# Round 0 of a token mixer with experts: peak, reciprocal and first spread of batch 3's state ahead of batch 1's correction on VectorE, the quadrant swap ahead of a transpose on TensorE

## What is computed

```python
h = relu(causal_conv(fake_quant(emb)[x]))                  # width 2
h = h + scan_mixer(layernorm(h))                           # below
h = h + expert_mlp(layernorm(h))                           # attn, fc1, gelu, fc2, next, gelu
...
log_x = log_matmul_exp(log_x0_I, log_cum)                  # linear recurrence x_t = A x_(t-1) + B u_t
c = jnp.max(log_x.real, axis=-1, keepdims=True)
x = jnp.exp(log_x - c + 2).real.reshape(Bsz, L, n * d)     # 4 heads of 64
y = jnp.matmul(x, C) + jnp.matmul(u, D)
```

## Time and profile before

| | us |
|---|---|
| median of 3 runs | 171.41 (171.39 to 171.44) |
| profiled execution, its time | 171.2 |
| its span | 169.5 |
| TensorE (matmul) busy | 160.5, 95% of the span |
| VectorE busy | 128.4, 76% |
| ScalarE busy | 101.7, 60% |
| GpSimd busy | 101.7, 60% |
| mean granted TensorE clock | 0.999 |

### The profile page before, as it was taken

One profiled execution on the slowest core, in us unless ns is written; L12 is line 12 of the kernel. 1 busy time (PEld: TensorE's weight loads), 2 busy tenths in 40 slices (PEclk: granted clock), 3 DMA queues, 4 the chain that ended last, 5 costly groups with the idle time before them and its releaser, 6 DMA issues.

```text
span 169.5 us, 3498 instructions
## 1 busy us (share of the span) xinstructions
PE 160.5 (95%) x1165; PEld 138.1 (81%) x1165; DVE 128.4 (76%) x403; ACT 101.7 (60%) x238; POOL 101.7 (60%) x168
## 2 busy tenths in 40 slices
PE   5977989999999999999999979999999999989992
PEld 1666875897765799987669979999999999989991
DVE  3979959833338384897995998989979898649893
ACT  3048999452233532423426947959779597788991
POOL 5337777669997134460313783996969969785000
PEclk9999999999999999999999999999999999999999
DMA  4996000000000000000000000010010100110022
GB/s 140 353 429 296 4 0 2 0 6 0 0 0 4 0 0 0 0 6 0 0 0 0 4 0 0 0 68 0 0 68 0 64 0 4 62 62 6 0 106 82
DMA packets 2182, 7.47 MB, mean 44 GB/s; under 512 B 238, under 2 KB 748, under 8 KB 1908
## 3 DMA queue, kind: packets, MB, share of 16 engines
q1 hardware_dynamic: 2146, 7.23, 11.2%
q10 hardware_dynamic: 18, 0.02, 0.1%
HBM read 5.15 MB, written 2.10 MB: 43 GB/s over the span
## 4 chain that ended last, share of the span: by engine, by line
PE 81%; DVE 6%; ACT 5%; POOL 3%; issue 3%; DMA 1%; POOLq 0%; ACTq 0%; DVEq 0%
PE bank L1358 12%; PE bank L1338 11%; PE bank L1287 8%; PE bank L1202 6%; PE bank L1196 5%; PE bank L1284 4%; PE bank L1066 4%; PE bank L1116 4%; PE bank L1307 4%; PE bank L1122 3%; PE bank L1314 2%; PE bank L1091 2%; PE bank L1039 2%; PE bank L1168 2%; DVE st L784 2%
## 5 line engine op out<-in xcount | busy, mean ns | idle before, releaser
L519 POOL TENSOR_TENSOR hid_p<-hid_f,hid_p 128x256 fp32r<-128x256 f32 x48 | 34.2, 739 | 14.2 <-ACT hid_p L713 14.2
L711 ACT ACTIVATE hid_f<-bank,pa 128x256 f32<-128x256 f32 x64 | 30.8, 491 | 15.6 <-PE bank L1338 14.2
L1338 PE MATMUL bank<-xaT_p,fc_p 128*128 128x256 f32 x192 | 35.0, 293 | 0.2 <-issue 0.2
L1358 PE MATMUL bank<-hid_p,out_hi 128*128 128x256 f32 x128 | 32.3, 289 | 0.5 <-POOL hid_p L519 0.5
L1338 PEld LDWEIGHTS bank<-xaT_p,fc_p 128*128 128x128 f32 x192 | 26.6, 189 | 0.4 <-issue 0.3
L1358 PEld LDWEIGHTS bank<-hid_p,out_hi 128*128 128x128 f32 x128 | 23.4, 188 | 1.3 <-POOL hid_p L519 0.7
L713 ACT ACTIVATE hid_p<-bank,pa 128x256 fp32r<-128x256 f32 x48 | 23.4, 487 | 0.0
L1287 PE MATMUL bank<-pb,xh 128*128 128x128 f32 x128 | 19.5, 275 | 0.0
L533 POOL TENSOR_TENSOR rstd<-spread,neg_half 128x8 f32<-128x8 f32 x8 | 13.6, 1696 | 8.9 <-DVE spread L976 8.9
L1358 PE MATMUL bank<-hid_p,out_lo 128*128 128x256 f32 x64 | 17.8, 278 | 0.0
L1287 PEld LDWEIGHTS bank<-pb,xh 128*128 128x128 f32 x128 | 16.9, 192 | 0.0
(11 more groups left out here) (161 smaller groups left out, 373.7 us busy)
## 6 DMA issues: line engine op xcount, KB each, us to landing
fc_w<-in_fc SPq DMA_DIRECT2D x2, 2048.0 KB, 11.7
out<-res SPq DMA_DIRECT2D x7, 256.0 KB, 2.0
pa<-in_pack_a SPq DMA_DIRECT2D x1, 407.0 KB, 3.2
pb<-in_pack_b SPq DMA_DIRECT2D x1, 384.0 KB, 4.5
out<-res SPq DMA_DIRECT2D x2, 128.0 KB, 1.7
pw<-in_pack_a SPq DMA_DIRECT2D x1, 64.0 KB, 3.8
emb_w<-in_emb SPq DMA_DIRECT2D x1, 62.5 KB
conv_w<-in_conv ACTq DMA_DIRECT2D x1, 1.0 KB
```

The source lines that it names most:

```text
L519: nc.gpsimd.tensor_tensor(hid_p[1][:, half, c, :], hid_f[:, m % HID_SLOTS, :], hid_p[0][:, half, c, :].bitcast(F32), ALU.subtract).then_in ...
L711: full = nc.scalar.activation(hid_f[:, m % HID_SLOTS, :], src, ACT.Gelu, bias=bias)
L1338: last = mm(fc1_bank(8 * b + n)[:, 0:HALF], fc1_p[w][:, e * HID + c * P:e * HID + (c + 1) * P], xaT_p[m][:, b % 2, half, :], start=(k == 0 ...
L1358: last = mm(out_bank(b, half)[:, half * HALF:(half + 1) * HALF], out_p[w][:, e, c * CH:(c + 1) * CH], hid_p[m][:, half, c, :], start=(c == ...
```

## The change

In round 0 alone, VectorE makes the peak, the reciprocal and the first of the two spreads of batch 3 right behind its maxima, ahead of the correction of batch 1's attended values. The second spread and the two scalings stay where they were. TensorE makes the swap of batch 3 ahead of the transposes of xa of batch 1. All other rounds stay as they are; the code of the three instructions is taken into two small functions. No instruction is added or removed.

```diff
--- before.py
+++ after.py
@@ -895,6 +895,22 @@
                                                     hid_p[0][:, half, c, :].bitcast(F32),
                                                     ALU.subtract).then_inc(hid_lo_dve, 1)
 
+                def reciprocals(b):
+
+                    if b == 0:
+                        dve.wait_ge(fc1_split, NE)
+                    dve.wait_ge(amax_ready, b + 1)
+                    dve.wait_ge(swap_done, b + 1)
+                    nc.vector.tensor_tensor(peak[:], amax[:, b % 2], bank_sw.rearrange("p (a i) -> p a i", a=NP),
+                                            ALU.max).then_inc(peak_ready, 1)
+                    dve.wait_ge(peak_ready, b + 1)
+                    chained(nc.vector.reciprocal(rcp[:], peak[:]))
+
+                def spread_reciprocal(a):
+
+                    return nc.vector.transpose(bank[a][:].rearrange("p (i k) -> p i k", k=NCH),
+                                               rcp[:, a, :].unsqueeze(2).broadcast_to([P, T, NCH]))
+
                 def late_residual(o):
 
                     dve.wait_ge(gel_ready, o + 1)
@@ -942,6 +958,9 @@
                                                            apply_absolute_value=True, apply_transpose=True)
                         last.then_inc(amax_ready, 1)
                     scan_part(j, "maxima")
+                    if j == 0:
+                        reciprocals(3)
+                        spread_reciprocal(0)
                     high_parts(j, range(0, 2))
                     if j == NB - 1:
                         late_residual(NB - 3)
@@ -980,18 +999,12 @@
                     b = j + 3
                     if b < NB:
                         g, bb = divmod(b, GB)
-                        if b == 0:
-                            dve.wait_ge(fc1_split, NE)
-                        dve.wait_ge(amax_ready, b + 1)
-                        dve.wait_ge(swap_done, b + 1)
-                        nc.vector.tensor_tensor(peak[:], amax[:, b % 2], bank_sw.rearrange("p (a i) -> p a i", a=NP),
-                                                ALU.max).then_inc(peak_ready, 1)
-                        dve.wait_ge(peak_ready, b + 1)
-                        chained(nc.vector.reciprocal(rcp[:], peak[:]))
+                        if j != 0:
+                            reciprocals(b)
                         scan_part(j, "reciprocal")
                         for a in range(NP):
-                            last = nc.vector.transpose(bank[a][:].rearrange("p (i k) -> p i k", k=NCH),
-                                                       rcp[:, a, :].unsqueeze(2).broadcast_to([P, T, NCH]))
+                            if (j, a) != (0, 0):
+                                last = spread_reciprocal(a)
                         chained(last)
                         scan_part(j, "spread")
                         if b >= 2:
@@ -1386,6 +1399,8 @@
                     fill(j, 1)
                     if j < 0:
                         fill(j, MIXER)
+                    if j == 0:
+                        swap_quadrants(scaled)
                     if 0 < attended < NB:
                         transpose_xa(attended)
                     if 0 <= mixed < NB:
@@ -1393,7 +1408,7 @@
                         mixer_out(mixed, 3)
                     if attended == 0:
                         transpose_xa(0)
-                    if scaled < NB:
+                    if scaled < NB and j != 0:
                         swap_quadrants(scaled)
                     fill(j, 2)
                     fill(j, 3)
```

## The result

| | before | changed |
|---|---|---|
| median, first timing (5 runs each) | 171.44 | 170.46 (170.03 to 170.71) |
| profiled execution | 171.2 | 170.71 |
| its span | 169.5 | 169.0 |

Two later executions, one of the kernel before and one of run 2, took some 885 us where all others took 169 to 174; they are left out of every comparison.

What follows compares the result with a forecast made beforehand. TensorE was taken as the bound from 100 us on, held ahead of that by its wait for xh; the stall's 1.19 us less 0.38 for late transposes of h gave 0.8 us won, 170.6 us, range 170.35 to 171.05.

Steps and rivals of the forecast that it cites:

- The stall's price: End of round 0: TensorE's wait for xh with its restart costs 3.35 - 2.16 = 1.19 us, the most to win.
- The delay of the transposes of h: Round 0: VectorE's correction starts 0.38 us later, and TensorE's transposes of h move one for one, to 93.57.
- The sum: End of round 0: 1.19 - 0.38 = 0.81 us won, TensorE's first mixer product for batch 3 at about 97.74.
- What sets the end: End of round 0: xh is ready by about 97.74, so TensorE's own lateness, not xh, sets the end.
- The swap without a wait on TensorE: Round 0: the swap, moved to 90.31, finds the maxima over at 89.80, with 0.5 us to spare.
- Its price on ScalarE's path: Round 0: the swap makes the xa transposes and ScalarE's reading of them 0.14 us later.
- L975's hold: VectorE's variance spread, 0.71 us, is held by GpSimd's subtraction; starting later it is held less, and L976's end stays.
- The lower bound: If the hand-over from swap to correction were hidden, 1.19 - 0.14 = 1.05 us would be won: 170.36 us.
- Its other term: Lower bound: with the hand-over hidden, only ScalarE's 0.14 us would remain as the delay.
- B: Moved instructions or next round cost more, VectorE held by GpSimd or xa transposes waiting: 170.9 to 171.1; chance 0.14.
- C: Gain taken back at the end, in round 5, by TensorE's wait for GpSimd's subtraction: no change, 171.4; chance 0.09.
- D: GpSimd's L519 series holds VectorE repeatedly, TensorE starts the mixer 0.4 us after today: 171.85; chance 0.05.

Runs made afterwards that it cites:

- run 2: The kernel before with only TensorE's half, the swap ahead of the xa transposes in round 0: 171.23 us against 171.43, ratio 0.9988.
- runs 8 and 10: The changed kernel with GpSimd's subtraction 3 ahead of its power in rounds 1 to 4, timed twice: 170.20 and 170.17 us, ratios 0.9930 and 0.9929.
- run 7: The changed kernel with the first spread moved behind the addition into h, ahead of its statistics: 170.52 us, ratio 0.9948 to the kernel before.
- run 3: The changed kernel with both spreads of batch 3 ahead of the correction in round 0: 170.93 us, ratio 0.9975 to the kernel before.
- run 6: The changed kernel with the swap back at its old place, so only VectorE's half: 172.19 us, ratio 1.0064 to the kernel before.
- run 4: The changed kernel with only peak and reciprocal ahead, both spreads behind the statistics: 170.59 us, ratio 0.9954 to the kernel before.
- run 12: Changed kernel, GpSimd's subtraction 3 first in rounds 1 to 4, round 0's swap behind the xa transposes, first spread behind the addition: 170.15 us, ratio 0.9920.
- run 5: The kernel before, unaltered, timed against itself and profiled again: 171.46 us against 171.48, ratio 1.0001.
- run 9: The changed kernel unaltered, a third time, against the kernel before: 170.43 us, ratio 0.9940.

## Why the prediction was right and wrong

Two terms of the sum failed, the price of the stall and the delay of the transposes of h; the mechanism, TensorE's own lateness and not xh, is the one that the runs show.

- **The stall's price: too small.** The step took 1.19 us, with a later round as the unheld measure (2.16). In three profiles of the changed kernel the distance is 2.09, 2.04 and 2.05 us, 2.06 on average, and in the two profiles of before it is 3.35 and 3.32, so the stall and its restart cost 1.27 us. The reference round had a wait of its own, for GpSimd, too short for the list of waits; runs 8 and 10 took it away, and the distance there fell to 2.08 to 2.10.
- **The delay of the transposes of h: too large.** The step said 0.38; it is 0.25, three times to the hundredth (4.94 against 4.69). The hand-over from swap to peak took 0.41, not 0.46, the first spread 0.64 to the next start, not 0.66; the correction started 0.30 late instead of 0.38, and its pair took 0.05 less, as the statistics did in run 7, which also stand right behind a spread there (0.83 against 0.87).
- **The sum** 1.27 - 0.25 = 1.02 us is what the traces give from the maxima to the end (81.01 on average against 79.98). Two small errors, 0.08 and 0.13, both to the low side, made 0.8 of it. All timed executions together, 17 of the changed kernel and 76 of before, have medians of 170.29 and 171.45: 1.16. The 0.1 us between 1.03 and 1.16 is not explained by any stretch of the profiles; it may be the scatter ahead of round 0, but the profiles do not show it: the maxima start at 88.72 on average in the three with VectorE's old order, at 88.69 in the other eleven. The ratio of the first timing, 1.2 us, lies high in the same way. With the 1.03 of the traces alone the median would be 170.38, just inside the range, so the two terms explain about half of the way from the forecast of 170.6 to 170.18; the other 0.2 us stays open.
- **What sets the end: right.** Xh was there first, and TensorE came late by the delay of h. With a delay of 0.25, 1.0 (run 3) and 2.04 us (run 6) the traces give a gain of 1.03, 0.35 and -0.77 us to the end of the span; 1.27 less the delay is 1.02, 0.27 and -0.77.
- **The swap without a wait on TensorE: right**, at 90.69 with the maxima over at 90.18. Its price on ScalarE's path was put at 0.14 and is 0.17.
- **L975's hold: right in kind.** It took 0.71 and 0.70 in the two profiles of before, 0.49 in run 2, 0.40 to 0.42 in the changed kernel and run 4, and 0.17 in runs 3, 6 and 7, where it began after GpSimd's pair had ended, and in run 12, where it began 0.11 us ahead of that end: the later it comes, the less it is held. In the changed kernel it ended at 95.61 and the pair (below) at 95.58. The rule of the Trainium skill ("SBUF — State Buffer", who interferes with whom) and the trace agree. L976's end stood 6.79 us behind the maxima against 6.85, so it hardly moved, as forecast, and xh was done 1.26 us sooner (8.74 us behind the maxima against 10.0; the step said 1.2).

```profile
94.12 1.46 POOL L519 TENSOR_TENSOR hid_p<-hid_f,hid_p 128x256 fp32r<-128x256 f32 x2 [0.39 <-ACT hid_p L713]
```

- **The bounds.** The lower bound, a hand-over that hides fully, was built on the 1.19 and so could not reach the 1.2 us of the first timing. Its other term, 0.14 for ScalarE alone, was too small as well: with no spread ahead at all (run 4) h is 0.24 late. A range must carry the error of its largest term; here that term had none.
- **The rivals.** B (held by GpSimd) did not come: peak and reciprocal took 0.19 and 0.35 beside L519. C (taken back at the end) did not come: in round 5 of the changed kernel the power still took 2.05 us and TensorE still waited 0.47 for the subtraction, its wait ending 3.49 us behind the power's start as before. D, the slower side, needed a delay of h above the stall's price; run 6 made one by the swap's place, not by GpSimd, and was slower by what the sum says.

## What to carry to other kernels

Work moved into an engine's idle time is free only up to the moment at which the idle time would have ended; from there it is paid by whatever the next instruction releases, and here that was the bottleneck engine itself. When the price of a stall is read as a difference between two rounds, look at the reference instruction by instruction first: a wait of 0.08 us showed in no list of waits here. And where executions differ ahead of the place of a change, count from an event just ahead of it: three profiles of the changed kernel agree to 0.1 us at the mixer and to 0.2 at the end that way, while their spans differ by 0.7.

## What was not expected of the hardware

The scatter of single executions of a program on one core is about 0.8 us from the fastest to the slowest (171.12 to 171.90 in run 5, 170.0 to 170.82 in run 9). In the profiled executions it arises far ahead of round 0. The statistics of the front part that start at 22.07 us in the profile of before start at 21.67 us in run 6 and at 22.71 in run 12; the maxima of batch 3 start at 88.50, 88.12 and 89.14. So the differences of 0.4 and 0.6 us are there at 22 us already and stay as they are up to round 0; in all fourteen profiles they change by less than 0.05 us between the two places. The DMA queues moved 278 and 240 GB/s in the first two stretches of 10 us and 1 in the third, so the scatter arises while the inputs are loaded. Which transfer or hand-over makes it was not singled out.

```profile
22.07 0.87 DVE L784 BATCH_NORM_STATS2 st<-h 128x6 f32<-128x128 f32 x4 [0.69 <-ACT h L619]
```

```profile
21.67 0.87 DVE L784 BATCH_NORM_STATS2 st<-h 128x6 f32<-128x128 f32 x4 [0.69 <-ACT h L619]
```
